# Moving the layer-norm steps to other pieces of a block in a one-core GNN and LSTM kernel

## The reference

```python
def _layernorm(x, axis=-1, eps=1e-05):
    m = jnp.mean(x, axis=axis, keepdims=True)
    v = jnp.var(x, axis=axis, keepdims=True)
    return (x - m) / jnp.sqrt(v + eps)
...
h = item_feat @ W_item.T + b_item                    # 10000 x 128
b = user_feat @ W_user.T + b_user                    # user_feat = layernorm(x), 10000 x 128
gnn = relu(adj @ h + b)                              # adj is 10000 x 10000, fp32
x = x + gnn
x = x + ffn(layernorm(x))                            # an LSTM over 10000 steps, then a gate, prefix and suffix sums
```

## Time and profile before

| what | value |
|---|---|
| median of 3 runs | 1440.17 us (1440.13 to 1441.91) |
| the profiled execution's own time | 1440.53 us |
| its span, first to last instruction | 1438.7 us |
| granted TensorE clock, mean | 0.995 |
| PE busy, of the span | 98% |
| DVE busy | 88% |
| ACT busy | 72% |
| POOL busy | 15% |
| moved by DMA | 442.96 MB, mean 308 GB/s |

### The profile page before, as it was taken

How to read it: one execution, slowest core, us unless ns; L and a number is a source line. 1 busy time by engine, 2 the same in 40 slices (tenths; PEclk the granted TensorE clock), 3 DMA queues, 4 the chain that set the end, 5 groups by cost and what they waited for, 6 DMA issues and landing times.

```text
span 1438.7 us, 26068 instructions
## 1 busy us (share of the span) xinstructions
PE 1412.5 (98%) x7418; PEld 1202.1 (84%) x7418; DVE 1270.6 (88%) x2081; ACT 1043.1 (72%) x1429; POOL 214.0 (15%) x189
## 2 busy tenths in 40 slices
PE   8999999999999999999999999999999999999995
PEld 7878888888888888788888788888888899999995
DVE  7999999999999999999999999999999766677667
ACT  6677777787777777777777777777777676556663
POOL 0000010000001001001001000100000132026776
PEclk9999999999999999999999999999999999999998
DMA  9999999999999999999999999999999403000003
GB/s 373 355 341 368 407 379 378 406 378 379 404 379 374 404 376 385 390 374 402 379 373 405 379 370 405 379 376 393 383 382 392 159 1 143 0 2 0 0 0 144
DMA packets 143466, 442.96 MB, mean 308 GB/s; under 512 B 23944, under 2 KB 43337, under 8 KB 143307
## 3 DMA queue, kind: packets, MB, share of 16 engines
q1 hardware_dynamic: 126048, 426.43, 77.2%
q10 hardware_dynamic: 17387, 16.14, 3.7%
HBM read 432.15 MB, written 10.36 MB: 308 GB/s over the span
## 4 chain that ended last, share of the span: by engine, by line
PE 88%; DVE 6%; DMA 3%; issue 2%; ACT 1%; SPq 0%; DVEq 0%; POOL 0%; ACTq 0%
PE psG L868 22%; PE psG L869 22%; PE psG L870 22%; PE psZ L964 9%; DVE a_lo L1180 3%; PE psZ L950 3%; PE psZ L952 3%; PE psZ L954 3%; DMA raw<-in_adj_main 2%; PE psG L889 1%; PE psZ L970 1%; PE psT L843 1%; PE psI L914 1%; ACT a_hi L653 1%; DVE u L1490 1%
## 5 line engine op out<-in xcount | busy, mean ns | idle before, releaser
L653 ACT ACTIVATE a_hi<-raw 128x1000 fp32r<-128x1000 f32 (+1 forms) x800 | 815.7, 1030 | 259.0 <-PE psG L870 211.6
L1180 DVE TENSOR_TENSOR a_lo<-raw,a_hi 128x1000 fp32r<-128x1000 f32 (+1 forms) x800 | 907.3, 1171 | 46.2 <-ACT a_hi L653 35.1
L868 PE MATMUL psG<-a_hi,item_hi 128*128 128x500 f32 x1560 | 623.5, 400 | 2.2 <-DVE item_lo L1213 1.0
L869 PE MATMUL psG<-a_lo,item_hi 128*128 128x500 f32 x1560 | 605.4, 388 | 0.0
L870 PE MATMUL psG<-a_hi,item_lo 128*128 128x500 f32 x1560 | 604.2, 387 | 0.0
L868 PEld LDWEIGHTS psG<-a_hi,item_hi 128*128 128x128 f32 x1560 | 293.0, 188 | 83.2 <-DVE a_lo L1180 20.2
L870 PEld LDWEIGHTS psG<-a_hi,item_lo 128*128 128x128 f32 x1560 | 292.9, 188 | 59.9
L869 PEld LDWEIGHTS psG<-a_lo,item_hi 128*128 128x128 f32 x1560 | 293.3, 188 | 56.8 <-issue 4.4
L964 PE MATMUL psZ<-hist,wh 128*128 (+1 forms) x1264 | 167.0, 275 | 2.9 <-DVE hist L1328 2.2
L964 PEld LDWEIGHTS psZ<-hist,wh 128*128 128x128 f32 x1264 | 154.0, 191 | 3.8 <-issue 2.4
L459 POOL TENSOR_TENSOR row_terms<-var,minus_half 125x4 f32<-125x4 f32 x20 | 37.5, 1878 | 628.5 <-DVE var L1136 628.5
(11 more groups left out here) (179 smaller groups left out, 821.6 us busy)
## 6 DMA issues: line engine op xcount, KB each, us to landing
raw<-in_adj_main SPq DMA_DIRECT2D x760, 500.0 KB, 6.8
raw<-in_adj_main SPq DMA_DIRECT2D x40, 250.0 KB, 4.8
sq<-rstd_copy ACTq DMA_DIRECT2D x20, 250.0 KB, 7.2
u<-x_copy SPq DMA_DIRECT2D x1, 5000.0 KB, 14.4
x_copy<-x1b SPq DMA_DIRECT2D x19, 250.0 KB, 7.2
sq<-rows_copy ACTq DMA_DIRECT2D x19, 250.0 KB, 6.0
un_bb<-rows_copy ACTq DMA_DIRECT2D x19, 250.0 KB, 7.8
u<-in_itemT SPq DMA_DIRECT2D x9, 512.0 KB, 9.7
```

The source lines that it names most:

```text
L653: nc.scalar.activation(a_hi[:, s % CUT, 0:n], raw[:, r % RAW, at:at + n], ACT.Copy)\
L868: pe.matmul(bank, w_hi, hi, start=(c == 0), stop=False)
L869: pe.matmul(bank, w_hi, lo, start=False, stop=False)
L1180: last = dve.tensor_tensor(a_lo[:, s % CUT, 0:m], raw[:, r % RAW, at:at + m], a_hi[:, s % CUT, 0:m].bitcast(f32), ALU.subtract)
```

## The change

One table of numbers is changed. No instruction is added or taken away; the order in which each engine issues them changes.

```diff
-AT = dict(relu=1, x1=2, scaled=3, bias=5, rows2=3, stats2=4, pair2=5, eps2=5, scale2=7, send2=8, spread2=12, apply2=16, shift2=17, out2=18,
-          rows1=11, stats1=12, pair1=13, eps1=13, send=15, spread=19, store=7, load=10, wx=12)
+AT = dict(relu=1, x1=2, rows2=3, stats2=4, pair2=5, eps2=5, scale2=7, send2=8, spread2=12, apply2=15, shift2=17,
+          out2=18, scaled=7, bias=9, rows1=10, stats1=11, pair1=12, eps1=12, send=14, spread=19, store=7, load=8, wx=12)
```

## The result

| | before | after |
|---|---|---|
| median | 1440.15 us (4 runs, 1439.42 to 1441.91) | 1430.01 us (4 runs, 1429.58 to 1431.52) |
| ratio after/before, 95% interval | | 0.9933 [0.9921, 0.9946] |
| span of the profiled execution | 1438.7 us | 1427.9 us |
| granted TensorE clock, mean | 0.995 | 0.996 |
| blocks 1 to 18 | 997.4 us | 985.9 us |

The change takes away 10.1 us, 0.7%. The forecast was 7.7 us, so the direction was right and the time lies inside the range, 2.5 us under the point and 0.5 above the range's lower end.

A forecast was written before the change was run, and what follows sets the result against it. PE was taken to be bound by thin margins behind DVE's `a_lo`. Terms 2.6 + 4.2 + 2.6 - 0.7 - 0.7 - 0.3 = 7.7 us gave 1432.5 us, range 1429.5 to 1438.

The forecast's parts named there:

- the rule: PE's first weight load of a half: PE loses the load's idle time less 0.15 us.
- The block's end: Halves 19.0 and 0.0: more margin removes PE's waits, giving back 2.6 and 4.2 us over 18 blocks.
- Pieces 3 to 5: Moving `scale_user` out of the crowded place removes the 10 waits at 5.0 and those hidden at 4.0: 2.6 us.
- the transfers: Halves late at 2.0 to 3.0: issued 0.49 us sooner, PE arrives 0.39 sooner; nothing counted.
- Pieces 6 to 8: After `scale_user` and `row_scale`, the load at 8.0 is 0.15 us late; 0.04 in 18 blocks: -0.7 us.
- The last block: `prepare` puts three more instructions ahead of 8.0, making the load 0.85 us late: -0.7 us, once.
- The terms' store: The store leaves 1.27 us later in PE's time, delaying the `a_hi` of 13.0; one block hurt: -0.3 us.
- Transfers as the bound: Landings at 2.0 do not move, PE waits out its lead: 3.5 us given back, 1436.0 us; chance 0.15.
- A larger stall at 8.0: Costlier `scale_user` and `row_scale`, or negative margin at 6.0: each block loses 0.27 us, 1436.6 us; chance 0.09.
- A later store: The terms' store lands 2 us later than counted, PE loses 1.1 at 13.0 in 19 blocks: 1453 us; chance 0.06.
- No gain at the block's end: Something just behind DVE also holds 19.0 and 0.0: 0.9 us gained, 1439.3 us, no change; chance 0.08.
- the best case of its range: 1429.5 us: no loss at 8.0, the store or the transfers, and their waits at 2.0 to 3.0 gone.

The follow-up runs named there:

- the one with 19 at 7.0: The changed kernel with `scaled` at 6 instead of 7; measured 1438.61 us, ratio to the kernel before 0.9966 [0.9955, 0.9976].

## Why the prediction was right, and where it was off

**What bounds the kernel.** That PE loses time where a margin is used up, and only there, holds in every run. The waits' cost by the rule, taken off the time of the blocks, leaves 985.6 to 986.5 us in all ten kernels. In before its 11.3 us are 4.4 at 0.0, 2.7 at 19.0, 2.6 at 5.0 and 1.6 at 2.0 to 3.0 and 14.0. Of the kernels with 19 waits at 0.0 none has blocks under 991; each without them is under 990, but for the one with 19 at 7.0.

**The block's end (2.6 + 4.2 predicted).** Right to 0.2 us. A block without other losses went from 55.16 (the mean of nine in before) to 54.77 (the mean in after): 0.39 x 18 = 7.0. The margins came out as counted: 0.54 at 16.0 and 18.0, 1.27 at 15.1, 0.29 at 19.0, 0.06 at 0.0. One step was told shorter than it is: the 0.49 gained at the addition is 0.54 against 0.05 at 18.0, but DVE's wait for ACT at 19.0 caps it at 0.29 there.

**Pieces 3 to 5 (2.6 predicted), and the transfers (0 predicted).** This is the step that failed. It split 4.0 us lost in pieces 2 to 5 into 1.4 for the waits at 2.0 to 3.0 and 14.0, "which stay", and 2.6 for `scale_user`. None stayed. Blocks 1 to 18 lost 11.5 us, of which 7.0 are the block's end and 4.5 these pieces: 1.9 more than the term. By the rule 1.4 to 1.6 of that are the waits that were to stay; the rest is that the sum took block 7, at 55.19 the longest of the nine undisturbed ones, for all of them, so that 4.0 us stood for 4.5. The sum had the move of the block's end give the late transfers nothing, since the halves are issued 0.49 sooner and PE arrives 0.39 sooner. Up to 0.1 that is what happened: half 2.0 is issued 4.56 us ahead of PE's 0.0 before and 4.57 after. The error is what was taken for granted behind it, that a transfer with the same start lands at the same time. Half 2.0 lands 1.4 us sooner against PE, halves 2.1 and 3.0 0.7 and 0.6. ACT's waits for transfers at 2.0 to 5.1 fell from 34.8 us to 9.0, and they fell in every kernel with a larger margin at the block's end. Why they land sooner is open.

The 2.6 for `scale_user` was the right size for its own waits: the 10 at 5.0 cost 2.6 by the rule in blocks 1 to 18, and they go when the scaling alone is moved. In the finished kernel the same move is worth only 0.9, since there few transfers are late and the crowded place has little to turn into waits. And the parts of the change do not add: undoing `rows1` to `send` alone costs 10.8 of the 11.5 us, undoing `apply2` alone 5.2, the scaling alone 0.9, together 16.9. From the other side, starting at the kernel with only the scaling moved (996.1): the multiplication's new place without the statistics' makes 996.7, nothing gained; the statistics' without the multiplication's 991.1, a gain of 5.0; both 985.9, a gain of 10.2 (`load`, which is moved along, is worth nothing by its own run). The statistics' new place gives the halves time to gain a margin, and the multiplication's spends it before the ceiling of 1.36 cuts it off (with `apply2` back the margin at 16.0 and 16.1 stands at 1.37 and 1.36).

**Pieces 6 to 8 (-0.7 predicted).** Over-sized. Half 8.0 in block 7 of after is the second of these loads:

```profile
435.17 0.19 PEld L870 LDWEIGHTS psG<-a_hi,item_lo 128*128 128x128 f32 x1
435.48 0.19 PEld L868 LDWEIGHTS psG<-a_hi,item_hi 128*128 128x128 f32 x1
435.61 0.19 PEld L869 LDWEIGHTS psG<-a_lo,item_hi 128*128 128x128 f32 x1
```

It starts 0.31 behind its forerunner instead of some 0.23: 0.08 late, where 0.15 was counted. `row_scale` took 0.07 of DVE's time (434.14 to 434.21 above), not the 0.14 of the sum. PE does not notice, by its timeline at the same place:

```profile
435.38 0.38 PE L870 MATMUL psG<-a_hi,item_lo 128*128 128x500 f32 x1
435.60 0.39 PE L868 MATMUL psG<-a_hi,item_hi 128*128 128x500 f32 x1
435.83 0.39 PE L869 MATMUL psG<-a_lo,item_hi 128*128 128x500 f32 x1
```

The matmuls start 0.22 and 0.23 apart. The prediction gave 0 to 0.05 per block and took 0.04; it is 0.

**The last block (-0.7 predicted).** Right: the idle time is 0.87 at 8.0, less 0.15 is 0.72. The block is 0.8 longer than before, 55.07 against 54.28; no wait shows the other 0.1.

**The terms' store (-0.3 predicted).** Over-sized: no wait at 13.0 in any block. From the store's issue to the broadcast's, ACT's timeline shows 10.9 to 13.0 us in the 19 blocks of before. In after it shows 10.5 to 10.6 in 12 blocks and 10.8 to 11.6 in seven; block 7 and block 10:

```profile
434.34 0.29 ACTq L615 DMA_DIRECT2D rows_copy<-row_terms  x1
...
444.86 0.33 ACTq L622 DMA_DIRECT2D sq<-rows_copy  x1
...
598.69 0.29 ACTq L615 DMA_DIRECT2D rows_copy<-row_terms  x1
...
610.26 0.33 ACTq L622 DMA_DIRECT2D sq<-rows_copy  x1
```

A value that repeats to 0.1 us is the place in ACT's list; the store had landed before. I had taken the store's time as fixed, and it is not. So 0.3 was counted for one block that never came.
The Trainium skill (DMA: Bandwidth & Descriptors, Latency and other measured facts) has HBM access at 2 us under high load, by which this term is 0. The term is 0, but not for that reason: block 10 above, where ACT's broadcast left 11.57 us behind the store, disagrees with 2 us.

**The rivals.** Transfers as the bound: refuted, and with the opposite sign, for the landings at 2.0 moved by more than PE did and ACT's waits for them halved. A larger stall at 8.0: refuted (no wait there outside the last block). A later store: its mechanism exists (the run with the terms sent later), but after the change the `a_hi` of 13.0 still starts 3.4 us or more ahead of PE's load, and 2.33 is needed. No gain at the block's end: refuted; nothing behind DVE held 0.0.

In sum: 7.7 + 0.2 (end) + 1.9 (pieces 2 to 5) + 0.7 (8.0) + 0.3 (store) - 0.1 (last block) = 10.7, against 10.8 in the span. All but the last of these errors point the same way, and most of their sum (the waits at 2.0 to 3.0, the load at 8.0, the store) is what the prediction had named as the best case of its range.

**What stays open:** why the terms' store is late in some blocks and not in others, and why the transfers of halves 2.0 to 5.1 take less time after the change though they are issued at the same place against PE.

## What to carry to other kernels

Where one engine feeds another with barely more speed, write down the margin step by step (so much gained per unit, so much lost per extra instruction, a ceiling set by the ring), and place extra work where the margin is full, well ahead of a place where it must be whole. Such a ledger was good to 0.07 us here, and told 7.0 of 11.5 us in advance. Then look at the loads of the next stretch, but at when they land and not only at when they are issued: here they started at the same place against PE and landed up to 1.4 us sooner. Moves of this kind do not add up, so undo them one at a time from the finished version as well as adding them to the old one: the multiplication's new place was worth 5.2 us in the one and nothing in the other.

## What the runs showed of the hardware

- A weight load that starts 0.08 us late costs PE nothing (half 8.0 above). With a longer wait PE loses the idle time less 0.15: a wait of 0.54 at 7.0 makes a block 0.38 longer, against 0.39 by the rule, and the same rule tells the blocks' time of all ten kernels to 0.6 us.
- A store of 3.9 KB in 16-byte pieces, next to adjacency at about 400 GB/s, held ACT's next broadcast to 10.9 us or more behind its issue in all 19 blocks of before, in 17 to more than 11.0, and in one to 12.99. In after it is issued 1.24 us later against PE's half 7.1 and did so to more than 11.0 in 5 of 19. The move of `xb`'s load is not the reason: with `load` back it still did in 9 of 19, and the times lie between 10.5 and 11.85. The cause is open.
- Half 2.0 of `raw` (500 KB) took 6.7 us from issue to landing in before and 5.4 in after, means of 18 blocks, issued at the same place against PE.
- The mean granted clock was 0.994 to 0.996 in the profiled execution of every kernel, so none of the differences is the clock's.
